# A four-layer graph network on one core: exponent levels for two heads at once, source rows by TensorE, degrees by VectorE

## The reference, cut to what matters

```python
# layer 1, graph attention with four heads
h = (x @ W).reshape(n, HEADS, C)
a_s = jnp.einsum('nhc,hc->nh', h, att_src)
a_d = jnp.einsum('nhc,hc->nh', h, att_dst)
e = jax.nn.leaky_relu(a_s[src] + a_d[dst], 0.2)
m = jax.ops.segment_max(e, dst, num_segments=n)
p = jnp.exp(e - m[dst])
z = jax.ops.segment_sum(p, dst, num_segments=n)
alpha = p / (z[dst] + EPS_SOFTMAX)
out = jax.ops.segment_sum(h[src] * alpha[:, :, None], dst, num_segments=n)
# layer 2, attention over the edges
e = jnp.sum(Q[receiver] * K[sender], axis=-1) * scale
w = jnp.exp(e - segment_max(e, receiver)[receiver])
attn = segment_sum(w[:, None] * V[sender], receiver) / segment_sum(w, receiver)
# layer 3 divides by the number of edges of a node
deg = jax.ops.segment_sum(jnp.ones((src.shape[0],), x.dtype), dst, num_segments=n)
```

## Time and profile before

| what | us |
|---|---|
| median of 3 executions (2929.94 to 2932.85) | 2930.45 |
| the profiled execution's own time | 2929.37 |
| its span | 2927.7 |
| TensorE, VectorE, ScalarE, GpSimd busy | 2393.8, 2007.1, 1787.0, 476.1 |
| attention sweep of layer 1, from its first load to its last copy | 1106.6 to 2090.0 |
| attention sweep of layer 2, from its first load to its last copy | 2169.9 to 2553.6 |

### The profile page before, as it was taken

The page is one execution under the profiler, slowest core; times in us unless marked ns, Lnnn a source line. Parts: engine busy times, 40 slices in busy tenths (PEclk is TensorE's granted clock), DMA queues, the critical chain, the costliest instruction groups (busy, mean ns, idle before and its releaser), DMA issues. The chain is left out here.

```text
span 2927.7 us, 62500 instructions
## 1 busy us (share of the span) xinstructions
PE 2393.8 (82%) x16906; PEld 1621.4 (55%) x16907; DVE 2007.1 (69%) x3577; ACT 1787.0 (61%) x4164; POOL 476.1 (16%) x825
## 2 busy tenths in 40 slices
PE   1988998988998954888888888888649999959795
PEld 1444444544544543666666666666527777735453
DVE  6777767777770026999999999998555555466175
ACT  1998989999990014766666667766338888610101
POOL 1444444444440000000000000000000000001010
PEclk7999999999999967999999999999869999979897
DMA  1222222222228605222222222222123333058193
GB/s 39 101 105 97 103 97 103 103 103 103 109 103 328 248 5 196 76 84 79 80 83 88 91 91 91 91 92 70 52 92 116 112 112 113 21 224 359 34 426 130
DMA packets 132818, 347.78 MB, mean 119 GB/s; under 512 B 14025, under 2 KB 115004, under 8 KB 115772
## 3 DMA queue, kind: packets, MB, share of 16 engines
q1 hardware_dynamic: 132544, 345.22, 31.7%
HBM read 218.96 MB, written 126.23 MB: 118 GB/s over the span
## 5 line engine op out<-in xcount | busy, mean ns | idle before, releaser
L434 PE MATMUL ps_build<-OH,KEY 128*128 128x400 bf16 x4108 | 737.0, 339 | 82.3 <-ACT KEY L391 44.0
L391 ACT ACTIVATE KEY<-KEY,cols 128x128 bf16<-128x128 bf16 x2054 | 622.0, 398 | 96.8 <-DVE KEY L362 95.7
L434 PEld LDWEIGHTS ps_build<-OH,KEY 128*128 128x128 bf16 x4108 | 399.9, 99 | 419.8 <-DVE OH L366 84.6
L1083 ACT ACTIVATE gr_e<-gr_ps,att_cols 128x256 f32<-128x256 f32 (+1 forms) x1300 | 502.0, 485 | 212.5 <-PE gr_ps L990 210.0
L362 DVE TENSOR_SCALAR KEY<-iota_key,key_base,cols 128x128 bf16<-128x128 int16 x1027 | 388.0, 410 | 220.4 <-PE ps_build L434 193.1
L990 PE MATMUL gr_ps<-ident,gr_r 128*128 128x128 f32 x2500 | 389.0, 296 | 100.2 <-DVE gr_r L1179 86.6
L409 POOL TENSOR_TENSOR KEY<-KEY,cols 128x256 bf16<-128x256 bf16 (+1 forms) x627 | 377.2, 602 | 496.8 <-DVE KEY L362 496.8
L990 PEld LDWEIGHTS gr_ps<-ident,gr_r 128*128 128x128 f32 x2500 | 291.4, 150 | 183.8 <-issue 136.9
L1019 PE MATMUL gr_ps<-gr_e,heads 128*33 128x128 f32 x5000 | 364.9, 277 | 25.5 <-DVE gr_e L1186 25.5
L1186 DVE SCALAR_TENSOR_TENSOR gr_e<-gr_e,gr_count_t 128x3072 f32<-128x3072 f32 (+1 forms) x104 | 349.5, 3361 | 36.1 <-ACT gr_count_t L1100 23.4
L1152 DVE CUSTOM_DVE_ANT_0 gr_unread<-gr_src_rows,gr_closed 128x3125 bf16<-128x3125 f32 (+1 forms) x100 | 344.4, 3444 | 19.6 <-DMA gr_src_rows<-gat_rows_d 15.2
(11 more groups left out here) (275 smaller groups left out, 1997.6 us busy)
## 6 DMA issues: line engine op xcount, KB each, us to landing
adjacency<-stage SPq DMA_DIRECT2D x200, 400.0 KB, 2.5
sage_ring<-count_by_source SPq DMA_DIRECT2D x50, 1600.0 KB, 8.8
agg_gcn_ring<-adjacency SPq DMA_DIRECT2D x25, 1600.0 KB, 8.4
gr_count<-adjacency SPq DMA_DIRECT2D x25, 1600.0 KB, 7.9
ar_counts<-adjacency SPq DMA_DIRECT2D x25, 1600.0 KB, 6.7
count_by_source<-gr_count_t SPq DMA_DIRECT2D x12, 3200.0 KB, 18.7
gr_src_rows<-gat_rows_d SPq DMA_DIRECT2D x4, 1600.0 KB, 19.5
fg_node<-gat_node_sums SPq DMA_DIRECT2D x1, 1650.0 KB, 6.3
```

The source lines that it names most:

```text
L391: last = act.activation(KEY[:, slot + j, v, :], KEY[:, slot + j, 0, :], ACT.Copy, scale=k.cols[:, 1 + v, bass.ds(c + j, 1)])
L434: last = pe.matmul(ps[:, 2 * (s % 2) + (v > 0), 0:SL], KEY[:, slot + j, v, :], OH[:, slot + j, :], start=slot == s % 2 * (BODY + 1) and j ...
L1083: last = act.activation(e[:, s, 0:w], ps[:, i % RINGS, c:c + w], ACT.Exp, bias=cols[:, h, s:s + 1])
```

## The change

Three edits in `gat_project`, `gat_rows` and `attend_rows`; names of buffers follow.

1. The source rows are no longer made in `gat_project`, stored and broadcast by transfers. ScalarE spreads each head's attention vector to 128 equal columns (`wide_watt`), and TensorE multiplies it with the transposed features in `gat_rows`, 8 pairs of matmuls for each of four heads, so that all 128 partitions of the result hold the head's row. ScalarE copies it from PSUM in halves. The transposed features therefore stay where the exponentials `e` will be.
2. `level` is made for a pair of heads, after the second's `best`: the same four instructions on 128x2x2 elements.
3. The degrees are summed by VectorE with `tensor_reduce`, after `keep`; ScalarE's `measure`, the copy of its result and the waits on it go.

```diff
 # gat_project
-            sp.wait_ge(rows_copied, 2)
-            sp.dma_start(rows_d, rows[:]).then_inc(stored, 16)
-            sp.wait_ge(stored, 16)
...
-            pe.wait_ge(copied, 2)
-            for b in range(NCW):
-                last = pe.matmul(ps[0:HEADS, b, 0:CW], watt[:, 0:HEADS], k.XT[:, b * CW:(b + 1) * CW], start=True, stop=True)
-            last.then_inc(rows_made, 1)
...
-            dve.tensor_scalar(rows[:, HALF:NP].rearrange("p (b c) -> p b c", c=CW), ps[0:HEADS, HB:NCW, 0:CW], 0.8, None,
-                              ALU.mult).then_inc(rows_copied, 1)
...
-            act.activation(rows[:, 0:HALF].rearrange("p (b c) -> p b c", c=CW), ps[0:HEADS, 0:HB, 0:CW], ACT.Copy,
-                           scale=0.8).then_inc(rows_copied, 1)
 # gat_rows
             load(0, 0)
-            sp.dma_start(src_rows[:, 0], rows_d[0].partition_broadcast(P)).then_inc(rows_in[0], 16)
             load(0, 1)
-            for h in range(1, HEADS):
-                sp.dma_start(src_rows[:, h], rows_d[h].partition_broadcast(P)).then_inc(rows_in[h], 16)
...
+            def source_rows(h):
+                for half in range(2):
+                    need(pe, rows_kept, 2 * h + half - 1)
+                    for b in range(HB):
+                        c = half * HALF + b * CW
+                        last = pe.matmul(ps[:, half * HB + b, 0:CW], wide_watt[:, h, :], XT[:, c:c + CW], start=True,
+                                         stop=True)
+                    last.then_inc(rows_made, 1)
+
+            pe.wait_ge(spread, 1)
+            for h in range(HEADS):
+                source_rows(h)
+            pe.wait_ge(rows_kept, 2 * HEADS)
             pe.matmul(ps[:, 7, 0:P], k.zeros[:, 0:P], k.zeros[:, 0:P], start=True, stop=True).then_inc(opened, 1)
...
+            act.wait_ge(set_up, 2)
+            act.activation(wide_watt[:], watt[:, 0:HEADS].unsqueeze(2).to_broadcast([P, HEADS, P]), ACT.Copy, scale=0.8
+                           ).then_inc(spread, 1)
+
+            def keep_rows(h):
+                for half in range(2):
+                    act.wait_ge(rows_made, 2 * h + half + 1)
+                    act.activation(src_rows[:, h, half * HALF:(half + 1) * HALF].rearrange("p (b c) -> p b c", c=CW),
+                                   ps[:, half * HB:(half + 1) * HB, 0:CW], ACT.Copy).then_inc(rows_kept, 1)
+
+            keep_rows(0)
+            mask(0, 0)
+            mask(0, 1)
+            for h in range(1, HEADS):
+                keep_rows(h)
             act.wait_ge(opened, 1)
-            act.wait_ge(set_up, 2)
-            for j in range(TWO):
-                mask(0, j)
             take_counts(0, 0)
...
-                    hold(dve, rows_in[h], 16, held)
+                    hold(dve, rows_kept, 2 * h + 2, held)
...
-                        level(g2, h2)
+                        if h2 % TWO:
+                            level(g2, h2 // TWO)
 
             for h in range(TWO):
                 for j in range(TWO):
                     best(0, h, j)
-                level(0, h)
+            level(0, 0)
 # attend_rows
             def load(t, u, lap):
-                hold(sp, weighed, t * 2 + 2, held_sp)
-                sp.wait_ge(measured, t + 1)
+                sp.wait_ge(weighed, t * 2 + 2)
...
-            def measure(t, u):
-                act.wait_ge(kept, t)
-                act.wait_ge(measured, t + RING)
-                act.activation(unread[:], counts[:, u, :], ACT.Copy, accum_out=deg_u[:, u % 2]).then_inc(measured, 1)
...
-                if exists(t, 2):
-                    measure(t + 2, (u + 2) % RING)
...
-                dve.wait_ge(measured, t + (RING + 1))
-                dve.tensor_copy(deg[:, bass.ds(t, 1)], deg_u[:, u % 2])
...
+            def measure(t, u):
+                dve.tensor_reduce(deg[:, bass.ds(t, 1)], counts[:, u % RING, :], AX_X, ALU.add)
...
                 keep(t, u)
+                if exists(t, 2):
+                    measure(t + 2, u + 2)
```

More of the change, by code:

```diff
@@ L759, in _, with gat_project @@
             act.wait_ge(x_turned, 1)
-            act.activation(k.XT[:], flat(ps), ACT.Copy)
-def gat_project(nc, k, heads, cols, rows_d):
+            act.activation(k.XT[:, 0:NP], flat(ps), ACT.Copy)
+def gat_project(nc, k, heads, cols, watt):
     with ExitStack() as ctx:
@@ L875, in gat_rows @@
         ps = ctx.enter_context(nc.psum_tensor("gr_ps", [P, 8, BANK], F32))
-        rows_in = [sem(f"gr_rows_in{h}") for h in range(HEADS)]
+        spread, rows_made, rows_kept = map(sem, ("gr_spread", "gr_rows_made", "gr_rows_kept"))
         loaded = [sem(f"gr_loaded{j}") for j in range(TWO)]
@@ L1153, in best, with level @@
                                          in1=closed[:, j, 0:n], scale=1.0, scalar=FLOOR, op0=ALU.subtract, op1=ALU.max,
[L1154 to L1156 removed]
+                                         accum_out=best_u[:, h % TWO, j:j + 1]).then_inc(bests, 1)
+            def level(g, pair):
                 w = width(g)
[L1158 removed]
+                hs = slice(TWO * pair, TWO * pair + TWO)
                 at = bass.ds(g * TWO, w)
[L1160 to L1162 removed]
+                a_d8 = cols[:, HEADS + TWO * pair:HEADS + TWO * pair + TWO, at]
+                a_d2 = cols[:, 2 * HEADS + TWO * pair:2 * HEADS + TWO * pair + TWO, at]
+                top = peak[:, :, 0:w]
+                done = (g * TWO + pair) * 3
+                dve.wait_ge(bests, g * (2 * HEADS) + (TWO * w * pair + TWO * w))
+                dve.tensor_tensor(top, best_u[:, :, 0:w], a_d8, ALU.add).then_inc(small, 1)
                 dve.wait_ge(small, done + 1)
[L1164 to L1165 removed]
+                dve.scalar_tensor_tensor(top, top, 0.2, top, ALU.mult, ALU.max).then_inc(small, 1)
                 dve.wait_ge(small, done + 2)
[L1167 to L1168 removed]
+                dve.scalar_tensor_tensor(floor_u[:, hs, 0:w], top, -1.25, a_d2, ALU.mult, ALU.add).then_inc(small, 1)
                 dve.wait_ge(small, done + 3)
[L1170 to L1171 removed]
+                dve.tensor_tensor(lift_u[:, hs, 0:w], floor_u[:, hs, 0:w], a_d8, ALU.add).then_inc(levelled, 1)
             def span(g, h):
@@ L1500, in _ @@
             raise_halves(0, 0)
-            measure(0, 0)
-            measure(1, 1)
             each_tile_of(act, step)
@@ L1550, in step @@
                 keep(t, u)
+                if exists(t, 2):
+                    measure(t + 2, u + 2)
             lowest(0, 0, 0)
+            measure(0, 0)
             lowest(0, 0, 1)
@@ L1557, in _ @@
             lowest(1, 1, 0)
+            measure(1, 1)
             each_tile_of(dve, step)
@@ L1802, in program @@
         with (nc.sbuf_tensor("heads", [P, HEADS, NT, C + 1], F32) as heads,
-              nc.sbuf_tensor("att_cols", [P, 3 * HEADS, NT], F32) as cols):
-            with nc.sbuf_tensor("XT_gcn", [P, NP], F32) as k.XT:
-                with nc.sbuf_tensor("agg0", [P, NP], F32) as agg:
-                    aggregate(nc, k, "agg_gcn", k.weight_rs, k.X, agg)
-                    finish_gcn(nc, k, agg)
-                gat_project(nc, k, heads, cols, rows_d)
-            gat_rows(nc, k, heads, cols, rows_d)
+              nc.sbuf_tensor("att_cols", [P, 3 * HEADS, NT], F32) as cols,
+              nc.sbuf_tensor("att_watt", [P, 2 * HEADS], F32) as watt,
+              nc.sbuf_tensor("exponentials", [P, NT, 2 * P], F32) as e):
+            k.XT = e[:].rearrange("p t c -> p (t c)")[:, 0:NP]
+            with nc.sbuf_tensor("agg0", [P, NP], F32) as agg:
+                aggregate(nc, k, "agg_gcn", k.weight_rs, k.X, agg)
+                finish_gcn(nc, k, agg)
+            gat_project(nc, k, heads, cols, watt)
+            gat_rows(nc, k, heads, cols, watt, e)
         finish_gat(nc, k)
```

36 lines of the change are left out of this document (11 added, 25 removed).

## The result

The changed kernel takes 2890.1 us (2888.5 to 2896.4, 4 runs) against 2930.6 (2929.9 to 2932.9, 4 runs): a ratio of 0.9865 with an interval of 0.9847 to 0.9882, or 40.4 us less. The prediction was 2887.5. The profiled execution took 2890.3 us, with a span of 2888.6, 39.1 less than before's 2927.7, so the balance by stage is made of spans.

A forecast was written before the change was run, and what follows sets the result against it. Bounds: VectorE in layer 1's sweep, a ring through ScalarE in layer 2's, a serial path between. Gains of 19 (degrees), 12 (levels) and 11.5 (source rows) sum to 42.5 us, forecasting 2887.5 us, range 2871 to 2904.

The forecast's parts named there:

- the first term: Layer 2's sweep: summing the degrees on VectorE gains .84 us a tile over 23 tiles, 19 us, bounds 12 to 20.
- The scores' own spacing: Layer 2, TensorE: a score's starts lie 2.69 us apart, .16 under its 2.85 busy; with 2.85 the gain is .52 a tile.
- The ring: Layer 2, TensorE's own sequence of work per tile: 13.79 us by the spacing of starts, against a period of 14.63.
- VectorE's own ring: Layer 2, VectorE's work and waits per tile: 12.8 us with the reduction at 3.48, 16.3 at twice that price.
- The rival in which VectorE becomes the bound: Layer 2: the reduction costs far more than 3.48 us; at 7.0 the period is 16.3 and the kernel 2945; chance 4%.
- That rival, drawn from the Trainium skill: Layer 2: TensorE, judged by weight loads, could run faster, gaining 42 us instead of 19, so 2864.5; chance 3%.
- Levels, 12 predicted: Layer 1's sweep: pairing levels gains 1.0 us a super-tile after head 2, 12 x 1.0 = 12 us, bounds 2 to 24.
- The swallowed half: Layer 1, after head 0: `span` starts 1.03 us earlier but the wait for counts grows from 1.57 to 2.6, gaining nothing.
- the second rival: Half of layer 2's gain, or none from levels because head 2's turns hold `span` back: 2894 to 2898; chance 8%.
- The rival in which both levels pay: Layer 1: the counts move with `span`, so the level after head 0 pays too, 12 us more, 2875.5; chance 4%.
- Source rows, 11.5 predicted: Between the layers: rows by TensorE bring the first turn of exponents at 1130.5 instead of 1141.71, 11.5 us gained.
- The rival of rows at half clock throughout: Prologue: TensorE stays at 1.2 GHz while making the rows, so +3 instead of -11.5, 2902; chance 10%.

The follow-up runs named there:

- only_deg: Kernel before the change with only the degrees summed by VectorE, levels and source rows as before: 2910.1 us, ratio 0.9934.
- only_pair: Kernel before the change with only the levels made in pairs, degrees and source rows as before: 2919.6 us, ratio 0.9957.
- only_rows: Kernel before the change with only the source rows made by TensorE, levels and degrees as before: 2919.5 us, ratio 0.9963.
- single23: Changed kernel with the levels of heads 2 and 3 made one by one again, heads 0 and 1 as a pair: 2889.8 us, one run.
- the counts come first: Changed kernel with TensorE turning the rest of the counts before head 0's first sums, not behind them: 2853.3 us, ratio 0.9739.
- row0_by_vector: Changed kernel with VectorE instead of ScalarE copying head 0's row from PSUM, and ScalarE's masks and copies reordered: 2882.5 us, one run.
- both: Changed kernel with the rest of the counts turned before head 0's sums and row 0 copied by VectorE: 2852.8 us, ratio 0.9735.

## Why the prediction held, step by step

- **The forecast's balance** was 19 + 12 + 11.5 = 42.5; 40.4 was measured by medians, 39.1 by spans. Each of the three mechanisms was shown by a run that holds it alone. That the first term came out to .3 us is in part luck, as the next point shows.
- **Layer 2, 19 predicted, 19.3 measured.** The scores' own spacing, .16 under their busy time, was the estimate that decided between 12 and 19: 2294.35 to 2297.04 is 2.69. The last turn takes .11, as taken. The ring came out at 13.69, .10 below the 13.79 of the sum. The reduction was 3.48, as interpolated, and the wait for the first exponential 1.70 for 1.75. A gain of .94 a tile would give 21.6 over 23 tiles; of the missing 2.3, 1.6 lie in the second-last tile, which grew from 13.21 to 14.85 us (from the copy of one tile's sum to the next). It has fewer scores to make, so TensorE waits 2.04 there for a take of ScalarE, and its clock falls:

```profile
2501.88 0.30 PE L1428 MATMUL ar_ps<-ident,ar_p 128*128 128x128 f32 x1 [2.04 <-ACT ar_pt L1482]
...
2502.01 4.69 PE L1438 MATMUL ar_ps<-ar_pt,X 128*128 128x128 f32 x26
```

```profile
2504.00:2507.00 3.00, 3.00 (x20) 3.00 (x20) 0.26 (x2) 0.00 (x0) 0.00 (x0) 0.64 0.00 0
```

  This loss isn't a price of the change. In only_deg, with the same code in this sweep, TensorE waited the same 2.04, the clock stayed at 1.00, and the tile took 13.23:

```profile
2521.43 0.30 PE L1420 MATMUL ar_ps<-ident,ar_p 128*128 128x128 f32 x1 [2.04 <-ACT ar_pt L1474]
2521.57 3.07 PE L1430 MATMUL ar_ps<-ar_pt,X 128*128 128x128 f32 x26
```

```profile
2521.00:2524.00 3.00, 2.56 (x23) 2.60 (x24) 1.99 (x5) 1.43 (x4) 0.00 (x0) 1.00 0.00 0
```

  So the term was booked too low, .84 a tile where .94 came, and the lower clock of this one execution hid most of that.

- **VectorE's own ring**, put at 12.8 with one reduction and 16.3 with two, was 16.12 with two. The rival in which VectorE becomes the bound needed 7.0 for the reduction; with 6.95 of them it gave 2952.7, close to its 2945. The advice of the Trainium skill ("VectorE: DVE Perf Modes", "Rules for kernel authors") against `tensor_reduce` is for one on a hot path. The second one was on it; the first, which hides, was not.
- **TensorE has no room** at 76% of weight loads: without any reduction the period was still 13.69. That rival, drawn from the Trainium skill ("Perfetto Trace Analysis", "Identifying the Most-Contended Engine"), falls; the spacing of the starts was the better witness.
- **Levels, 12 predicted, 9.7 measured.** This term was the one mis-sized. The price of a level, 1.03 as the rows said, was booked for twelve super-tiles. Ten of them gave .96 on average (9.6), super-tile 0 gave .8 and super-tile 11 nothing: for super-tile 12 it makes one `best` a head instead of two, and `span` of head 3 waits for TensorE's turns there, .44 us before the change and 1.64 after. By themselves the levels are thus worth 10.4, as only_pair measured. The last .7 of the 9.7 is a growth of super-tile 11 (68.25 to 68.97) that isn't shown to be the levels' doing. The clock was at half for a stretch of it, and so it was in only_rows, whose levels are single and whose super-tile 11 took 69.00. One window of each, the changed kernel's first:

```profile
1984.00:1987.00 3.00, 2.39 (x11) 2.39 (x12) 3.00 (x2) 1.22 (x4) 0.00 (x0) 0.50 0.00 0
...
1994.00:1997.00 3.00, 3.00 (x15) 3.00 (x16) 3.00 (x1) 1.89 (x5) 0.00 (x0) 0.50 0.00 0
```

  A 128x4 instruction costs .16 as a 128x2 one does: booking nothing for the width was right. The swallowed half is shown three times over: the wait of 2.68 where 2.6 was predicted, single23's unchanged time, and its 1.0 once the counts come first. The turns of head 2 didn't hold `span` back, as a part of the second rival had it: step 2 kept its 1.12. The rival in which both levels pay fell; with the counts first, the level after head 0 pays as well.
- **Source rows, 11.5 predicted.** The first turn came 12.1 us earlier, at 35.9 us where 37 was forecast; 10.9 of it is left by super-tile 1, beside the .8 of the level, and only_rows, which has no pairs, gained 11.0 there. (The recorded chain ends at 1130.5, which against 1141.71 makes 11.2 and not 11.5.) The step not foreseen is that super-tile 0's `weigh_rest` waits 2.24 us for the counts, which in before's prologue it did not; 1.44 of that belongs to the rows, as only_rows shows, and the other .8 to the level that went after head 0. Inside the term two sizes were a little high: the first half row could be copied 4.4 us after its matmuls began (1096.91 to 1101.35) where 5.0 was taken for it, and the two masks took 5.80 for 6.0. All else in the chain, the spread, the order of copies and masks, and the counts' 2.81, came as written. The fall of the clock between rows 1 and 2 came after 3.31 us of idling, forecast 3.6. Without the idling it didn't come (row0_by_vector, both), but in single23 it didn't come with it either, so the idling is needed for it as far as these runs show, and not enough. The rival of rows at half clock throughout fell: the two groups of 32 records took 12.5 and 12.7 us, 25.2 in all, and not 43.

The sum missed by 2.1 us against the median. By spans 3.4 are missing: 1.6 of the levels, .7 of super-tile 11's clock, .6 of the source rows and a start 2.0 later, against .3 more in layer 2 and 1.2 saved elsewhere; no part of the change explains the start or the 1.2.

## What to carry to other kernels

Price a removed instruction by what waits next on its engine: the same level was worth 1.0 us at one place and nothing at another, and the wait that swallowed it was itself worth 28 us in the loop and went with two lines in another order on TensorE. In a loop of several engines, write down every engine's ring with the starts of its own instructions, not their busy time, since the second-longest ring tells how much work can be moved onto an engine for nothing. When a loop gets faster, look at its first and last turns as well: there other engines are the bound. And before a microsecond of one execution is put down to the change, look for the same code in the other kernels' traces: here 1.6 us in layer 2 turned out to be the clock's, and the .7 in super-tile 11 also came with unchanged levels.

## What the hardware showed that was not expected

- The same wait of TensorE brought the clock down in some executions and not in others. In the second-last tile of layer 2 it waits 2.04 us in nine kernels: in seven of their profiles the 26 matmuls behind it took 4.69 or 4.70 us, in only_deg and both 3.07. In the prologue it stands still for 3.31 us in eight kernels: the 32 records behind it took 11.01 us in single23, 12.71 in four profiles and 13.83 to 13.90 in three. What decides between them isn't shown. A stretch of .47 us there cost nothing in both kernels that had it.
- Reductions of 3200 float32 columns cost 3.48 us, 1.04 ns a column beside a small fixed part, on the line through the reductions of 256 and 896 columns in the earlier trace rows.
- Two loads of a tile's counts that were issued together landed 3.8 us apart in the changed kernel (the adds behind them start at 1102.83 and 1106.63), where with a broadcast row between them it was 8.1.
